# Attention over 16 images: row shifts of the scores by two DMAs through DRAM, maxima of every fourth query

## The chip, the cores and the metric

One Trainium2 chip, one of its cores. The time is the device time of that core in microseconds (us) for one execution of the whole program, all 16 images; the median of several executions counts. Where a profile is read, times are from the start of its span.

## What is computed

For each of 16 images (1024 tokens of 512 channels): group norm in 32 groups, SiLU, a projection to q, k and v (8 heads of 64), softmax attention for each head over all 1024 tokens, an output projection, a bias, and the image added again. Cut to what matters:

```
xn = silu(group_norm(x, scale, offset))              # b, 32, 32, 512
q, k, v = split(einsum('bxyc,cd->bxyd', xn, w_qkv))  # 8 heads of 64
q = q * 64 ** -0.5
attn = softmax(einsum('bhdi,bhdj->bhij', q, k), axis=-1)
out = einsum('bhij,bhdj->bhid', attn, v)
out = einsum('bxyd,dc->bxyc', out, w_out) + b_out
return out + x
```

## The kernel before

Products are made in fp16 halves: a value is kept as a high fp16 and a low fp16 part, and the high and low terms are added by further matmuls. Scores stand as keys x queries, so the maximum of a query's row of scores can't be taken from them. The kernel therefore makes a cheap copy of the scores ahead, queries x keys, from the high parts alone, and takes each query's maximum from it. The maximum, negated and scaled, is then fed into the score matmuls as one more operand: 64 rows of the moving operand `QK2` hold the shift of each query, against 64 stationary rows that hold the constant `ROWC`, and so exp() gets shifted scores.

The work of an image is 64 units of TensorE work (`UNITS`), in 4 steps of 16 (`step`, u = 0 to 15); v = 16 x step + u. A head has 8 units: 4 for queries 0 to 511 (half 0) and 4 for queries 512 to 1023 (half 1). In every unit TensorE does, in program order:

- `scores` (L1107, L1108): four matmuls of 512 columns into one of two PSUM buffers `ST`. At every fourth unit it first waits for the shift of its half (L1103);
- `turn`, in nine units of the 64: transposes;
- in even units `times_v` (L1137, 18 short matmuls for probabilities times v, two units behind), then a block of maxima (L1019), then the first half of a side job (L1005, a projection of q, k, v or out, six matmuls); in odd units the block of maxima, the other half of the side job, and `times_v` last;
- the shift, when there is one, at the very end of the odd unit.

A block of maxima is two matmuls of 512 columns into the PSUM tile `TP`, 128 queries x 1024 keys. It runs `TOP_LEAD` = 6 units ahead of its head. VectorE reduces it to one column of `mx` (L782). There is one `TP`, so each use of it waits until VectorE drained the one before (L1011). After the fourth block of a half (u = 1, 5, 9 or 13) VectorE makes the column form of the shift, `ms` (L752, 128 x 4). TensorE, at the end of the same unit, waits for it and turns the four columns into rows by four matmuls with `ident16` into `TP` (L1026). VectorE copies 64 rows of that, 64 x 512, into `QK2` (L786), at the start of its next unit. The first scores that need it are three units behind the block of maxima: the fourth block of half 0 comes in unit 8h - 3 and its scores in unit 8h, the one of half 1 in 8h + 1 and 8h + 4. So 16 shifts for an image, 256 in all.

VectorE also takes the low part of half of the probabilities (L835, every unit; GpSimd takes the other half, L509), drains the side jobs (L723, L728, L735), and does the norm and half of the SiLU of the next image, mostly in step 2 (L796, L825, L828). ScalarE takes two exponentials a unit (L620, L623).

SyncE issues all DMAs, in the order of its own program: `load_x` (L367), `load_res` (L373), `store` (L379), `place` (L390) and `move_v` (L396), each behind its waits. An instruction that waits holds all that stand behind it. `place` issues six DMAs of 256 KB each that lay the q and k of the next two heads from `QK` into `QK1` and `QK2`; it stands at u = 7 of each step and waits for the side job that VectorE drains in unit 8. The maxima of the next pair of heads, from u = 10, wait for its first three.

`Count` follows the counts of the semaphores through the order of the uses; `TOPS` are the uses of `TP`.

Of the kernel before, what the change touches and what calls it, by code (L numbers as in the profile page):

```python
# [13 lines left out]
P = 128  # L14
# [6 lines left out]
HALF = 512  # L21
# [34 lines left out]
def unit_max(step, u, last=False):  # L56

    head, qb = divmod(16 * step + u + TOP_LEAD, TB)
    return [] if last and head == HEADS else [("max", head // 2 % 4, head % 2, qb)]


def unit_shift(step, u, last=False):

    return [("shift", pair, hh, qb // 4) for _, pair, hh, qb in unit_max(step, u, last) if qb % 4 == 3]
# [8 lines left out]
def shift_before(step, u, last=False):  # L73

    if u > 0:
        return unit_shift(step, u - 1, last) + unit_stats(step, u - 1, last)
    return unit_shift(step - 1, 15, last) + unit_stats(step - 1, 15, last) if step > 0 else []

# [56 lines left out]
def image_of(use, b, step):  # L135
# [3 lines left out]
    if use[0] == "out" or (use[0] == "ot" and step == 0):  # L139
# [3 lines left out]

JOBS_PROLOGUE = [("qk", 0, "qk"[i % 2], i // 2) for i in range(4)] + [("v", t) for t in range(TB)]
PROLOGUE = ([("mean",), ("var",)] + JOBS_PROLOGUE[:4]
            + [use for t in range(TB) for use in [("v", t)] + ([("shift", 0, 0, 0)] if t == 6 else [])
               + ([("max", 0, 0, t - 2)] if t >= 2 else [])])
TOPS = ("max", "shift", "mean", "var")
IMAGE_JOBS = [x for s in range(4) for u in range(0, 16, 2) for x in unit_job(s, u)]
HI_PARTS = ("qk", "v")  # L150

# [1 line left out]
class Count:  # L153


    PER_IMAGE = {"side": len(IMAGE_JOBS), "hi": sum(x[0] in HI_PARTS for x in IMAGE_JOBS),
                 "top": HEADS * (TB + 2) + 2, "shifts": 2 * HEADS}

    def __init__(self, side=0, hi=0, top=0, shifts=0, ring=0, mark=None, shifted=(0, 0)):
        self.side, self.hi, self.top, self.shifts, self.ring = side, hi, top, shifts, ring  # L160
        self.shifted = list(shifted)
        self.mark = dict(mark or {"qk": 0, "v": 0})

    def passed(self, use):
        if use[0] in TOPS:
            self.top = self.top + 1
            if use[0] == "shift":
                self.shifts = self.shifts + 1
                self.shifted[use[3]] = self.top
# [12 lines left out]
    def later(self, images):  # L182

        n = {name: images * per for name, per in self.PER_IMAGE.items()}

        return Count(self.side + n["side"], self.hi + n["hi"], self.top + n["top"], self.shifts + n["shifts"],
                     self.ring, {kind: at + n["side"] for kind, at in self.mark.items()},
                     [at + n["top"] for at in self.shifted])


assert len(ring_of()) % 2 == 0 and B % 2 == 0
# [8 lines left out]
def conv_attention(nc, x, gamma, beta, w_qkv, w_out, b_out, out):  # L200
# [4 lines left out]
    with ctx:  # L205
# [11 lines left out]
        ident16 = sb("ident16", [P, P], F16)  # L217
# [56 lines left out]
        x_first = [x_in[:], z[:], th[:], Ph[:, 0:2, :].rearrange("p a n -> p (a n)").bitcast(F32).rearrange(  # L274
            "p (t c) -> p t c", t=2)]

        ST = ps("ST", [P, 2, 2 * HALF], F32)
        PV = ps("PV", [P, 512], F32)
        SD = ps("SD", [P, 512], F32)
# [44 lines left out]
        xn_lo = sem("xn_lo")  # L324
        v_moved = sem("v_moved")
        shift_ready = sem("shift_ready")
        scores_ready = sem("scores_ready")
        exp_done = sem("exp_done")
        lo_dve = sem("lo_dve")
# [19 lines left out]
        def _(sp):  # L349
# [31 lines left out]
            def place(pair, cnt):  # L381
# [15 lines left out]

            def step(b, s, cnt, first=False, last=False):
                for u in range(16):
                    if u % 2 == 0:  # L400
                        for use in unit_job(s, u, first, last):
                            cnt.passed(use)
                    if s == 0 and not last:
                        if u == 0 and first:
                            load_x(b + 1, 0)
                        if u in (1, 3, 7):
                            load_x(b + 1, (1, 3, 7).index(u) + 1)
                    if s == 0 and u == 4:
                        move_v(b)
                    if s == 1 and u == 0 and not first:  # L410
                        load_res(b - 1, 7)
                    if s == 2 and u == 4:
                        for t in range(4):
                            load_res(b, t)
                    if u == 7 and not (last and s == 3):
                        place((s + 1) % 4, cnt)
                    if s == 3 and u == 14 and not isinstance(b, int):
                        load_x(b + 2, 0)
                    if u % 2 == 1:
                        for use in unit_job(s, u, first, last):  # L420
                            if use[0] == "out":
                                store(b - 1, use[1], cnt.side)
                                if 1 <= use[1] <= 3:
                                    load_res(b - 1, use[1] + 3)

            cnt = Count()
            for use in JOBS_PROLOGUE:
                cnt.passed(use)
                if use == ("qk", 0, "k", 1):
                    place(0, cnt)  # L430
            step(0, 0, cnt, first=True)
            step(0, 1, cnt, first=True)
            with nc.Fori(0, B // 2 - 1, engines=[sp.engine], hint_back_edge=True) as two:
# [259 lines left out]
        def _(dve):  # L693
# [61 lines left out]
            def top_use(use, image, cnt):  # L755
# [12 lines left out]
                elif use[0] == "var":  # L768
# [11 lines left out]
                elif use[0] == "max":  # L780
# [65 lines left out]
            def step(b, s, par, cnt, first=False, last=False):  # L846
                turned = []
                for u in range(16):
                    v = 16 * s + u
                    if (s, u) == AGGREGATE_AT and not last:  # L850
                        dve.wait_ge(bn_done, b + 2)
                    for use in (shift_before(s, u, last) if not (first and v == 0) else []):
# [31 lines left out]
            nc.vector.tensor_copy(ident16[:], ident32[:])  # L884
# [114 lines left out]
        def _(pe):  # L999
# [9 lines left out]
            def top_use(use, image, cnt):  # L1009

                wait(pe, top_drained, cnt.top)  # L1011
                if use[0] == "max":
                    _, pair, hh, qb = use
                    slot = head_slot(pair, hh)
                    if qb == 0:

                        pe.wait_ge(placed[hh], PLACED * (4 * image + pair + 1))
                    for kh in range(2):
                        ins = nc.tensor.matmul(TP[:, bass.ts(kh, HALF)], QK1[:, slot, 0, bass.ts(qb, P)],  # L1019
                                               QK1[:, slot, 1, bass.ts(kh, HALF)], start=True, stop=True)  # L1020
                if use[0] == "shift":
                    _, pair, hh, half = use
                    pe.wait_ge(shift_ready, cnt.shifts + 1)
                    for i in range(4):
                        qb = 4 * half + i
                        ins = nc.tensor.matmul(TP[:, bass.ts(i, P)], ms[:, hh, qb:qb + 1].to_broadcast([P, P]),  # L1026
                                               ident16[:], start=True, stop=True)
                if use[0] == "mean":
                    pe.wait_ge(chan_stats, image + 1)
                    ins = nc.tensor.matmul(TP[:, 0:CC], group_mean[:], mv[:, :, 0], start=True, stop=True)  # L1030
# [63 lines left out]
                else:  # L1094
                    pe.wait_ge(ot_lo, 4 * (b - 1 if n == 3 else b) + n + 1)

            def scores(b, v, slot, cnt):
# [43 lines left out]
            def step(b, s, par, cnt, first=False, last=False):  # L1141
                for u in range(16):
                    v = 16 * s + u
                    before = (b, v - 2) if v >= 2 else (b - 1, UNITS + v - 2)
                    wait_ring(("score", v), b, first, last)
                    scores(b, v, cnt.next_slot(), cnt)
                    for use in unit_turn(s, u, first, last):
                        wait_ring(use, b, first, last)
                        turn(use, image_of(use, b, s), cnt.next_slot(), x_in)
# [7 lines left out]
                    else:  # L1157
# [81 lines left out]
```

## Time and profile before

| | us |
|---|---|
| median of 3 runs | 3889.32 |
| lowest and highest | 3886.81 and 3890.93 |
| the profiled execution, its own time | 3886.07 |
| its span, first to last instruction | 3884.3 |

Of the profile the page's busy shares of the engines matter, the view of waits (who waited for whom, in total and how many times), the groups of instructions by line and form (busy, mean ns of one, idle time of the engine before them), the timelines of TensorE (PE), its weight loads (PEld), VectorE (DVE) and SyncE's DMA queue (SPq), the windows (busy time of each engine in a stretch), and the DMAs with their time from issue to landing. The rows themselves stand below.

### The profile page before, as it was taken

To read this page: it belongs to the slowest core of one execution; us is meant where nothing else is said; L and a number is where in the kernel's file an instruction comes from. 1 tells how busy PE (TensorE), PEld (TensorE's weight loads), DVE (VectorE), ACT (ScalarE), POOL (GpSimd) and SP (SyncE) were. 2 spreads that over 40 slices of the span, in tenths; PEclk is the share of its full clock that TensorE was granted. 3 is DMA by queue.
4 is the path that set the end of the run, shared out by engine and by line. 5 is a ranking of instruction groups with operands and counts; after the bars stand their busy time and mean duration, and the time that the engine had idled before them with its cause. 6 is when DMAs were issued, how large, how long until landed. Compare 5 with 4: busy or idle time off the path is not lost. (4 is left out here: it accounts for less than half of the span.)

```text
span 3884.3 us, 92365 instructions
## 1 busy us (share of the span) xinstructions
PE 3643.0 (94%) x32844; PEld 2099.6 (54%) x32844; DVE 3349.9 (86%) x4378; ACT 2811.0 (72%) x3074; POOL 1766.9 (45%) x1739
## 2 busy tenths in 40 slices
PE   4889999999999999999999999999999999998997
PEld 2555555555555555555555555555555555555553
DVE  6888989889898898888888898888988989888885
ACT  3777777777777777777777777777777777777774
POOL 1353544445444444544535444344444444444444
PEclk7999999999999999999999999999999999999999
DMA  2212212132121222213122121221212222131220
GB/s 89 60 30 80 58 49 70 33 88 56 50 78 39 67 56 69 58 39 86 37 80 59 49 69 38 81 56 50 77 39 67 56 69 58 40 85 37 61 61 33
DMA packets 120769, 228.84 MB, mean 59 GB/s; under 512 B 12672, under 2 KB 29056, under 8 KB 120320
## 3 DMA queue, kind: packets, MB, share of 16 engines
q1 hardware_dynamic: 120320, 222.87, 21.2%
q8 instruction: 279, 4.57, 0.5%
q14 instruction: 170, 1.39, 0.1%
HBM read 71.57 MB, written 33.55 MB: 27 GB/s over the span
## 5 line engine op out<-in xcount | busy, mean ns | idle before, releaser
L509 POOL TENSOR_TENSOR Pl<-P,Ph 128x512 f16<-128x512 f32 x1024 | 1238.3, 1209 | 1703.9 <-ACT Ph L623 1691.0
L620 ACT ACTIVATE P<-ST,cns 128x1024 f32<-128x1024 f32 x1024 | 1141.0, 1114 | 899.3 <-PE ST L1108 883.4
L782 DVE TENSOR_REDUCE mx<-TP 128x1 f32<-128x1024 f32 x1024 | 1246.3, 1217 | 164.5 <-PE TP L1019 156.8
L623 ACT ACTIVATE Ph<-ST,cns 128x1024 f16<-128x1024 f32 x1024 | 1133.8, 1107 | 0.0
L835 DVE TENSOR_TENSOR Pl<-P,Ph 128x512 f16<-128x512 f32 x1024 | 978.8, 956 | 11.5 <-ACT Ph L623 7.3
L1137 PE MATMUL PV<-V,Ph 128*128 128x129 f16 (+2 forms) x10240 | 862.1, 210 | 3.9 <-DVE Pl L835 1.4
L1137 PEld LDWEIGHTS PV<-V,Ph 128*128 128x128 f16 x10240 | 772.0, 97 | 124.9 <-ACT pv_sum L631 8.8
L1137 PE MATMUL PV<-V,Pl 128*128 128x65 f16 x8192 | 834.8, 192 | 0.0
L1137 PEld LDWEIGHTS PV<-V,Pl 128*128 128x128 f16 x8192 | 723.0, 98 | 109.1 <-issue 0.6
L1108 PE MATMUL ST<-QK 128*128 128x512 f16 x2048 | 778.2, 380 | 2.6 <-issue 2.6
L1107 PE MATMUL ST<-QK 128*128 128x512 f16 x2048 | 778.6, 380 | 0.2 <-ACT Ph L623 0.2
L1005 PE MATMUL SD<-X,wq 128*128 128x512 f16 x3048 | 745.5, 381 | 15.9 <-POOL X L496 15.2
L1019 PE MATMUL TP<-QK 128*128 128x512 f16 x2048 | 611.0, 380 | 27.7 <-DVE QK L786 13.7
L1005 PEld LDWEIGHTS SD<-X,wq 128*128 128x128 f16 x3048 | 291.1, 98 | 395.4 <-DVE QK L723 34.9
L1005 PE MATMUL SD<-wo,OT 128*128 128x512 f16 x1536 | 376.8, 383 | 44.8 <-DVE QK L723 27.4
L1005 PE MATMUL SD<-wq,X 128*128 128x512 f16 x1488 | 361.6, 379 | 10.2 <-DVE V L728 7.2
L1107 PEld LDWEIGHTS ST<-QK 128*128 128x128 f16 x2048 | 202.8, 99 | 184.1 <-issue 3.0
L1108 PEld LDWEIGHTS ST<-QK 128*128 128x128 f16 x2048 | 200.6, 98 | 182.4 <-issue 2.5
L1005 PEld LDWEIGHTS SD<-wo,OT 128*128 128x128 f16 x1536 | 145.8, 98 | 244.9 <-DVE res L735 39.0
L786 DVE CAST QK<-TP 64x512 f16<-64x512 f32 x256 | 176.1, 688 | 116.5 <-PE TP L1026 113.7
L723 DVE SCALAR_TENSOR_TENSOR QK<-SD,sc,QK 128x512 f16<-128x512 f32 x254 | 190.0, 748 | 91.6 <-ACT QK L577 75.0
L519 POOL TENSOR_TENSOR O<-pv_sum,den 128x256 f32<-128x256 f32 x256 | 157.8, 616 | 239.8 <-DVE pv_sum L843 239.8
(105 smaller groups left out, 2872.8 us busy)
## 6 DMA issues: line engine op xcount, KB each, us to landing
QK<-QK SPq DMA_DIRECT2D x384, 256.0 KB, 4.8
res<-in_x SPq DMA_DIRECT2D x128, 256.0 KB, 2.8
out<-res SPq DMA_DIRECT2D x128, 256.0 KB, 2.0
x_in<-in_x SPq DMA_DIRECT2D x61, 512.0 KB, 3.8
V<-V SPq DMA_DIRECT2D x16, 1040.0 KB, 6.3
V<-in_L_conv_w_qkv SPq DMA_DIRECT2D x4, 768.0 KB, 10.2
P<-in_L_conv_w_out SPq DMA_DIRECT2D x1, 1024.0 KB, 13.9
z<-in_x SPq DMA_DIRECT2D x1, 512.0 KB, 5.6
```

Of the source, the lines that this page charges most:

```text
L509: nc.gpsimd.tensor_tensor(Pl[:, v % 4, HALF:], P32[:, v % 2, HALF:], Ph[:, v % 4, HALF:], ALU.subtract).then_inc(lo_pool, 1)
L620: nc.scalar.activation(P32[:, v % 2, :], ST[:, slot, :], ACT.Exp, scale=cns[:, 0:1])
L623: nc.scalar.activation(Ph[:, v % 4, :], ST[:, slot, :], ACT.Exp, scale=cns[:, 0:1]).then_inc(exp_done, 1)
L723: nc.vector.scalar_tensor_tensor(out=QK[:, lo, cols], in0=bank, scalar=sc[:, col:col + 1], in1=QK[:, hi, cols], op0=ALU.mult, op1=ALU.subt ...
L782: nc.vector.reduce_max(mx[:, hh, qb:qb + 1], TP[:], AX.X).then_inc(top_drained, 1)
L786: nc.vector.tensor_copy(QK2[r, head_slot(pair, hh), 0, bass.ts(half, HALF)], TP[r, 0:HALF]).then_inc(top_drained, 1)
L835: nc.vector.tensor_tensor(Pl[:, v % 4, 0:HALF], P32[:, v % 2, 0:HALF], Ph[:, v % 4, 0:HALF], ALU.subtract).then_inc(lo_dve, 1)
L1005: ins = nc.tensor.matmul(bank, stationary(i, c), moving(j, c), start=(c == 0 and i + j == 0), stop=(c == CC - 1 and i == 1))
L1019: ins = nc.tensor.matmul(TP[:, bass.ts(kh, HALF)], QK1[:, slot, 0, bass.ts(qb, P)], QK1[:, slot, 1, bass.ts(kh, HALF)], start=True, stop=True)
L1107: nc.tensor.matmul(dst, QK1[:, at, 1, kb], QK1[:, at, 0, bass.ts(q, HALF)], start=True, stop=False)
L1108: ins = nc.tensor.matmul(dst, QK2[:, at, 1, kb], QK2[:, at, 0, bass.ts(q, HALF)], start=False, stop=True)
L1137: ins = nc.tensor.matmul(PV[:, cols], stationary, moving, start=kb == qb == n == 0, stop=kb == TB - 1, skip_group_check=True)
```

## The change

The shift no longer goes over TensorE, PSUM and VectorE. The uses `shift` of `TP` go, with their four matmuls, the copy L786, `ident16` and the counts kept for them. SyncE, once `ms` is there, writes the four columns of `ms` into a row of 512 fp16 in DRAM (128 pieces of 8 bytes), waits for that, and reads the row from DRAM into the 64 rows of `QK2` (64 rows of 1 KB). The scores wait for the second DMA in place of the copy. It stands in SyncE's program at the unit in which the fourth block of the half is made.

So that the row in DRAM is in the order of the queries when partition p writes its four values side by side, a block of maxima now holds every fourth query of its half: partition p of block i is query 4p + i. The stationary operand of the two matmuls of a block is thus read with a step of four elements instead of one.

```
 def place_shift(b, n):                                   # new, SyncE
     head, half = n // 2 % HEADS, n % 2
     pair, hh = head // 2, head % 2
     sp.wait_ge(shift_ready, 2 * HEADS * b + n + 1)
     sp.dma_start(rows[half].rearrange("(p j) -> p j", j=4), ms[:, hh, 4 * half:4 * half + 4]
                  ).then_inc(shift_row[half], 16)
     sp.wait_ge(shift_row[half], 16 * HEADS * b + 16 * (n // 2) + 16)
     sp.dma_start(QK2[rows_of(1 - hh), head_slot(pair, hh), 0, bass.ts(half, HALF)],
                  rows[half:half + 1].to_broadcast([HD, HALF])).then_inc(shift_placed[half], 16)
```

```
@@ SyncE, step @@
                 if s == 3 and u == 14 and not isinstance(b, int):
                     load_x(b + 2, 0)
+                for n in unit_shift(s, u, last):
+                    place_shift(b, n)
                 if u % 2 == 1:
@@ VectorE, top_use @@
-                else:
-                    _, pair, hh, half = use
-                    r = rows_of(1 - hh)
-                    nc.vector.tensor_copy(QK2[r, head_slot(pair, hh), 0, bass.ts(half, HALF)], TP[r, 0:HALF]
-                                          ).then_inc(top_drained, 1)
@@ TensorE, top_use @@
-                        ins = nc.tensor.matmul(TP[:, bass.ts(kh, HALF)], QK1[:, slot, 0, bass.ts(qb, P)],
+                        ins = nc.tensor.matmul(TP[:, bass.ts(kh, HALF)],
+                                               QK1[:, slot, 0, qb // 4 * HALF + qb % 4:(qb // 4 + 1) * HALF:4],
                                                QK1[:, slot, 1, bass.ts(kh, HALF)], start=True, stop=True)
-                if use[0] == "shift":
-                    _, pair, hh, half = use
-                    pe.wait_ge(shift_ready, cnt.shifts + 1)
-                    for i in range(4):
-                        qb = 4 * half + i
-                        ins = nc.tensor.matmul(TP[:, bass.ts(i, P)], ms[:, hh, qb:qb + 1].to_broadcast([P, P]),
-                                               ident16[:], start=True, stop=True)
@@ TensorE, scores @@
-                    pe.wait_ge(top_drained, cnt.shifted[q])
+                    pe.wait_ge(shift_placed[q], 16 * HEADS * b + 16 * head + 16)
@@ TensorE, step, end of odd units @@
-                        for use in unit_shift(s, u, last):
-                            top_use(use, b, cnt)
```

## Rows read from the trace of the kernel before

**Rows 1.** Page: span, busy time of the engines, granted TensorE clock in 40 slices.

```profile
span 3884.3 us, 92365 instructions
...
PE 3643.0 (94%) x32844; PEld 2099.6 (54%) x32844; DVE 3349.9 (86%) x4378; ACT 2811.0 (72%) x3074; POOL 1766.9 (45%) x1739
...
PEclk7999999999999999999999999999999999999999
```

**Rows 2.** View of waits, whole span: us in total, times, longest.

```profile
PE TP L1026 <- DVE ms L752: 98.0, 98, 3.0
...
PE TP L1019 <- DVE QK L786: 13.7, 30, 1.9
PE TP L1019 <- DVE mx L782: 12.6, 16, 2.0
```

**Rows 3.** Groups by form: count | busy us, mean ns | idle before, by whom ended.

```profile
L786 DVE CAST QK<-TP 64x512 f16<-64x512 f32 x256 | 176.1, 688 | 116.5 <-PE TP L1026 113.7
...
L1019 PEld LDWEIGHTS TP<-QK 128*128 128x128 f16 x2048 | 157.4, 97 | 156.2 <-DVE mx L782 52.9 <-DVE QK L786 17.4 <-issue 1.0
...
L1079 PEld LDWEIGHTS ST<-ident,O 128*128 128x128 f32 x512 | 61.1, 144 | 17.9 <-issue 3.4 <-POOL O L519 2.0 <-ACT Ph L623 1.0
```

**Rows 4.** TensorE's timeline at a shift without a wait: start, length in us.

```profile
2001.62 0.19 PE L1137 MATMUL PV<-V,Pl 128*128 128x65 f16 x1
2001.67 0.40 PE L1026 MATMUL TP<-ident,ms 128*128 128x128 f16 x4
2001.90 0.38 PE L1107 MATMUL ST<-QK 128*128 128x512 f16 x1
2002.12 0.38 PE L1108 MATMUL ST<-QK 128*128 128x512 f16 x1
```

**Rows 5.** TensorE's timeline in step 2, from u = 5 to u = 8.

```profile
2116.41 0.59 PE L1019 MATMUL TP<-QK 128*128 128x512 f16 x2
...
2120.41 0.40 PE L1026 MATMUL TP<-ident,ms 128*128 128x128 f16 x4 [1.39 <-DVE ms L752]
...
2127.24 0.38 PE L1107 MATMUL ST<-QK 128*128 128x512 f16 x1
```

**Rows 6.** VectorE's timeline at the same shift.

```profile
2118.11 1.22 DVE L782 TENSOR_REDUCE mx<-TP 128x1 f32<-128x1024 f32 x1
2119.37 0.98 DVE L752 TENSOR_SCALAR ms<-mx,cns 128x4 f16<-128x4 f32 x1
2120.84 0.68 DVE L786 CAST QK<-TP 64x512 f16<-64x512 f32 x1 [0.49 <-PE TP L1026]
```

**Rows 7.** Windows: a stretch of step 2; length, then PE, PEld, DVE, ACT, POOL busy.

```profile
2134.00:2150.00 16.00, 14.66 (x145) 8.43 (x144) 15.24 (x19) 12.97 (x16) 7.11 (x7) 1.00 0.26 62
```

**Rows 8.** DMA issues: count, KB each, median us from issue to landing.

```profile
res<-in_x SPq DMA_DIRECT2D x128, 256.0 KB, 2.8
out<-res SPq DMA_DIRECT2D x128, 256.0 KB, 2.0
...
bet<-in_L_conv_gn_offset SPq DMA_DIRECT2D x1, 2.0 KB, 3.8
```

**Rows 9.** SyncE's timeline in step 1: the six DMAs of `place`, and a store.

```profile
2069.97 5.93 SPq L390 DMA_DIRECT2D QK<-QK  x6
2076.40 0.88 SPq L379 DMA_DIRECT2D out<-res  x1
```

**Rows 10.** Landing of the sixth DMA of that `place`, issued at 2074.72.

```profile
L390 SPq DMA_DIRECT2D QK<-QK x1: 1186/1186/1186, 2074.7 to 2074.7; - x1
...
DMA to landing us min/median/max: 5.4/5.4/5.4
```

**Rows 11.** Landing of that store.

```profile
DMA to landing us min/median/max: 4.3/4.3/4.3
```

**Rows 12.** VectorE's timeline in step 1, u = 9.

```profile
2074.07 0.23 DVE L752 TENSOR_SCALAR ms<-mx,cns 128x4 f16<-128x4 f32 x1
```

**Rows 13.** TensorE's timeline in step 1: first scores of u = 12.

```profile
2081.43 0.38 PE L1107 MATMUL ST<-QK 128*128 128x512 f16 x1
```

More of the change, by code:

```diff
@@ L62, in unit_shift, with head_of @@
 def unit_shift(step, u, last=False):
-    return [("shift", pair, hh, qb // 4) for _, pair, hh, qb in unit_max(step, u, last) if qb % 4 == 3]
+    return [2 * head_of(step, u) + qb // 4 for _, pair, hh, qb in unit_max(step, u, last) if qb % 4 == 3]
+def head_of(step, u):
+    return (16 * step + u + TOP_LEAD) // TB
 def unit_stats(step, u, last=False):
@@ L70, in unit_stats, with stats_before @@
     return [(kind,)] if kind and not last else []
[L73 to L77, printed above, removed]
+def stats_before(step, u, last=False):
+    return unit_stats(step, u - 1, last) if u > 0 else unit_stats(step - 1, 15, last) if step > 0 else []
 JOBS = [["qk"] * 4 + ["out"] * 4, ["qk"] * 4 + ["out"] * 4, ["qk"] * 4 + ["v"] * 4, ["qk"] * 4 + ["v"] * 4]
@@ L145 @@
 PROLOGUE = ([("mean",), ("var",)] + JOBS_PROLOGUE[:4]
-            + [use for t in range(TB) for use in [("v", t)] + ([("shift", 0, 0, 0)] if t == 6 else [])
-               + ([("max", 0, 0, t - 2)] if t >= 2 else [])])
-TOPS = ("max", "shift", "mean", "var")
+            + [use for t in range(TB) for use in [("v", t)] + ([("max", 0, 0, t - 2)] if t >= 2 else [])])
+TOPS = ("max", "mean", "var")
 IMAGE_JOBS = [x for s in range(4) for u in range(0, 16, 2) for x in unit_job(s, u)]
@@ L156, with __init__ @@
     PER_IMAGE = {"side": len(IMAGE_JOBS), "hi": sum(x[0] in HI_PARTS for x in IMAGE_JOBS),
[L157 to L161, printed above, removed]
+                 "top": HEADS * TB + 2}
+    def __init__(self, side=0, hi=0, top=0, ring=0, mark=None):
+        self.side, self.hi, self.top, self.ring = side, hi, top, ring
         self.mark = dict(mark or {"qk": 0, "v": 0})
@@ L166, in passed @@
             self.top = self.top + 1
-            if use[0] == "shift":
-                self.shifts = self.shifts + 1
-                self.shifted[use[3]] = self.top
             return
@@ L184, in later @@
         n = {name: images * per for name, per in self.PER_IMAGE.items()}
-        return Count(self.side + n["side"], self.hi + n["hi"], self.top + n["top"], self.shifts + n["shifts"],
-                     self.ring, {kind: at + n["side"] for kind, at in self.mark.items()},
-                     [at + n["top"] for at in self.shifted])
+        return Count(self.side + n["side"], self.hi + n["hi"], self.top + n["top"], self.ring,
+                     {kind: at + n["side"] for kind, at in self.mark.items()})
 assert len(ring_of()) % 2 == 0 and B % 2 == 0
@@ L275, in conv_attention @@
             "p (t c) -> p t c", t=2)]
+        rows = nc.dram_tensor("shift_rows", (2, HALF), F16, kind="Internal").ap()
         ST = ps("ST", [P, 2, 2 * HALF], F32)
@@ L326, in conv_attention @@
         shift_ready = sem("shift_ready")
+        shift_row = [sem(f"shift_row{half}") for half in range(2)]
+        shift_placed = [sem(f"shift_placed{half}") for half in range(2)]
         scores_ready = sem("scores_ready")
@@ L430, in _ @@
                     place(0, cnt)
+            place_shift(0, 0)
             step(0, 0, cnt, first=True)
@@ L779, in top_use @@
                                             ALU.mult, ALU.add).then_inc(guess_ready, 1)
-                elif use[0] == "max":
+                else:
                     _, pair, hh, qb = use
                     nc.vector.reduce_max(mx[:, hh, qb:qb + 1], TP[:], AX.X).then_inc(top_drained, 1)
-                else:
-                    _, pair, hh, half = use
-                    r = rows_of(1 - hh)
-                    nc.vector.tensor_copy(QK2[r, head_slot(pair, hh), 0, bass.ts(half, HALF)], TP[r, 0:HALF]
-                                          ).then_inc(top_drained, 1)
                 cnt.passed(use)
@@ L851, in step @@
                         dve.wait_ge(bn_done, b + 2)
-                    for use in (shift_before(s, u, last) if not (first and v == 0) else []):
+                    for use in stats_before(s, u, last):
                         top_use(use, b + 1, cnt)
@@ L883, in _ @@
             dve.wait_ge(const_ready, 5)
-            nc.vector.tensor_copy(ident16[:], ident32[:])
             dve.wait_ge(gn_loaded, 32)
@@ L1018, in top_use @@
                     for kh in range(2):
-                        ins = nc.tensor.matmul(TP[:, bass.ts(kh, HALF)], QK1[:, slot, 0, bass.ts(qb, P)],
+                        ins = nc.tensor.matmul(TP[:, bass.ts(kh, HALF)],
+                                               QK1[:, slot, 0, qb // 4 * HALF + qb % 4:(qb // 4 + 1) * HALF:4],
                                                QK1[:, slot, 1, bass.ts(kh, HALF)], start=True, stop=True)
-                if use[0] == "shift":
-                    _, pair, hh, half = use
-                    pe.wait_ge(shift_ready, cnt.shifts + 1)
-                    for i in range(4):
-                        qb = 4 * half + i
-                        ins = nc.tensor.matmul(TP[:, bass.ts(i, P)], ms[:, hh, qb:qb + 1].to_broadcast([P, P]),
-                                               ident16[:], start=True, stop=True)
                 if use[0] == "mean":
@@ L1095, in wait_ring, with scores @@
                     pe.wait_ge(ot_lo, 4 * (b - 1 if n == 3 else b) + n + 1)
-            def scores(b, v, slot, cnt):
+            def scores(b, v, slot):
                 head, q, kp = v // 8, v // 4 % 2, v % 4
@@ L1145, in step @@
                     wait_ring(("score", v), b, first, last)
-                    scores(b, v, cnt.next_slot(), cnt)
+                    scores(b, v, cnt.next_slot())
                     for use in unit_turn(s, u, first, last):
```

1 line of the change is left out of this document (removed).

## The prediction

> **What bounds the kernel now.** I read the page first: the reader is to see that TensorE is busy for 94% of the span at the full granted clock, and VectorE for 86% [rows 1]. So TensorE's order sets the time, and what matters is its own work and its 241 us of idle time (3884.3 - 3643.0). Then the view of waits: of that idle time 98.0 us in 98 pieces is spent at the shift, waiting for `ms`, the largest single entry; another 13.7 us in 30 pieces is a block of maxima that waits for the copy of the shift out of `TP` [rows 2]. Then the timelines around shifts. In one without a wait the four matmuls push the next scores back by 0.23 us (2001.67 to 2001.90) [rows 4]. In one with a wait TensorE has nothing to do for 1.39 us [rows 5], because VectorE reached the block of maxima late: reduce at 2118.11, `ms` ready at 2120.35, 3.9 us after the block's matmuls began at 2116.41 [rows 5, 6]. Last the windows: in a 16 us stretch of step 2 VectorE is busy 15.24 us and TensorE 14.66 [rows 7]. There VectorE is no spare engine but nearly a second bound.
>
> **What goes from TensorE.** (a) 256 shifts at 0.23 us: 59 us [rows 3, 4]. (b) The wait for `ms`, 98 us, and with each of these 98 pieces the tail of the last matmul before it: that one is drawn 0.19 us long while its successor would start 0.05 us later, so a break costs 0.14 us more than its idle time; 98 x 0.14 = 14 us [rows 2, 4]. Together 112. (c) The blocks that wait for the copy: 13.7 us + 30 x 0.14 = 18 us [rows 2, 4]. The sum is 189 us.
>
> **What goes from VectorE.** 256 copies of 688 ns, 176 us, and 116.5 us in which it stood before them, waiting for TensorE's four matmuls [rows 3]. That is 1.1 us at each shift on average. By itself it is worth nothing, as VectorE is not the bound over most of the image, but it decides how much of (b) lasts. After (b) TensorE no longer waits for a late VectorE at `ms`; the next place where it can be late is the next block of maxima, which needs the same `TP` drained. There TensorE is ahead by 0.23 + 0.14 + the wait of about 1.0 us, 1.4 us in all, and VectorE by 0.68 + 0.49 = 1.17 us at a shift such as the one shown [rows 2, 4, 6]. The difference, 0.2 to 0.3 us, can come back as a wait: 98 x 0.3 = 29 us. I take the 29, with 0 as the low end (a stall of TensorE elsewhere lets VectorE catch up) and 60 as the high end.
>
> **What the new path costs.** Nothing of it runs on TensorE or VectorE; it is latency behind `ms` and in front of the scores three units on. Both ends of that interval have rows. `ms` ready at 2120.35, scores at 2127.24: 6.9 us [rows 5, 6]. Ready at 2074.30, scores at 2081.43: 7.1 us [rows 12, 13]. In the middle images no shift has less. With the change the scores come earlier by the 0.23 us of the four matmuls, and by the wait of that shift with its 0.14: 6.9 - 0.23 - 1.39 - 0.14 = 5.1 us for the worst, 6.9 us for the second.
>
> The chain has two DMAs. The first writes 1 KB to DRAM in 128 pieces; the nearest rows are the stores to DRAM, 2.0 us for 256 KB, and from above the 3.8 us of `bet`, 512 pieces of 4 bytes that was issued right behind a 512 KB load [rows 8]. I take 2.0, because the time of a small DMA is latency and `bet` had a load before it. The second reads 64 KB from DRAM; the nearest row is `res<-in_x` with 2.8 us for 256 KB, four times as much [rows 8]; I take 2.3, bounds 2.0 and 2.8. With 0.1 us for SyncE to go on, the chain is 4.4 us (bounds 4.1 and 6.7). It fits into 5.1 us and more: twelve of the sixteen shifts of an image are hidden. If the cover is gone, each 0.1 us over it costs 0.1 us of TensorE.
>
> The other four, at u = 9 of each step, meet `place`. Its six DMAs are issued over 5.93 us from 2069.97, and the sixth (2074.72) lands 5.4 us later, at 2080.1 [rows 9, 10]. A store issued at 2076.40, which alone takes 2.0 us, took 4.3 us and landed at 2080.7, 0.6 us behind the sixth [rows 8, 9, 11]: the queue is served in its order. The first DMA of the shift will do the same: landed at 2080.7, second issued 2080.8, landed 2083.1, but wanted at 2081.43 - 0.23 = 2081.2. A stall of 1.9 us. That is the worst of the four; in steps 0, 2 and 3 the same reckoning, averaged over the middle images, gives 0.1, 0.9 and 1.1 us, and 1.6 for step 1: 3.7 us an image, 58 us in all. Bounds: 30 us with 2.0 us for each DMA and 0.3 us behind `place`, 100 us with 2.5 and 2.8.
>
> What is queued behind the waits on SyncE: SyncE now waits inside `place_shift` for `ms` and for the first DMA, 2 us or 4 at u = 9. Behind it stand stores and loads of `res` with many us of cover, `load_x` (in step 3 it now goes behind two shifts, some 3 us before its transposes), and `place`, three units behind the shift of u = 5, which is done in about half of that. I cost these at nothing; the cover is one to two units of about 3.5 us each.
>
> The strided weights: a block's weight load takes 97 ns, hidden under matmuls of 512 columns; no row has a strided one. The nearest is the fp32 load, 144 ns [rows 3]. Up to the 0.22 us from one matmul of 512 columns to the next [rows 4] it stays hidden except the first load behind the short matmuls of `times_v`, in even units: 512 x (144 - 97) ns = 24 us at most. I take 0, since the fp32 load moves twice the bytes and this one the same. A gain is excluded: no read becomes shorter. The Trainium skill speaks against this edit on one page (TensorE: Matmul & The Clock Gate, section Weight-path perf modes): a fast weight load reads 32 bits at a time, two fp16 values, and with a step of four only one of the two is wanted. The same table lets strided chunks keep the mode, which is what I take; no row here shows it. On the DMA pair the page DMA: Bandwidth & Descriptors (Anatomy of one DMA) gives about 2.0 us plus bytes / 436 GB/s; an estimate by it is 4.2 us for the chain, against 4.4 by the rows, and its specifications say that pieces under 512 B are read, changed and written again, which would lengthen the first.
>
> **The sum**, against the profiled execution's 3886.1 us (2 us over its span): 3886 - 189 + 29 + 58 = 3784. The median of the runs lies 3 us above the profiled one, so I say 3786.
>
> **The rivals.** 1. All of the chain is hidden, because stalls and VectorE's lag overlap and the DMAs are quick: 3886 - 189 + 0 + 12 to 30, 3709 to 3727. For it: two DMAs at 2.0 us leave the queue's tail as the only cost. Against: [rows 9 to 11] show that tail at 0.6 us more. 2. The gain mostly given back: first DMA 3.0, second 2.8, 1 us behind `place`. Then also the shifts in steps 2 and 3 with 5.1 to 5.5 us are late; 147 us of stalls, 3886 - 189 + 147 + 10 = 3854. 3. Slower: the first DMA is like `bet`, 3.8 us (or 2 us behind `place`), the second 2.8, 6.7 us in all. At u = 9 TensorE then stalls for 2.8 us on average and at the other twelve for 0.4: 16 x (4 x 2.8 + 12 x 0.4) = 256 us, less 189: 3953. It turns from gain to loss where the lone chain reaches about 6.0 us. For it: 8-byte pieces, which no row shows. Against: the latency of 2.0 us for 256 KB. 4. The strided load is slow: each load above 215 ns is bare twice in a block. It needs (215 + 102 / 2048 x 1000 = 265) ns a load to eat the gain; at 390, four times today's, 2048 x 175 ns = 358 us, so 4140. No row is near it. 5. VectorE becomes the bound of step 2 and TensorE's waits only move to blocks and side jobs: (b) lasts for the 34 waits outside step 2 alone, so about 64 x 1.1 = 70 us more come back: 3854. Against: VectorE loses 1.1 us at each shift too. 6. That the change doesn't take the four matmuls away: excluded by the diff.
>
> **How the numbers follow.** Forecast (3750 to 3820) 0.60; rival 1 0.12; rivals 2 and 5 (3820 to 3875) 0.16; rival 3 0.07; rival 4 0.03; about no change, between 2 and 3, 0.02. The likeliest alone gives 3750 to 3820; the range that holds 8 in 10 takes in part of rivals 1 and 2 and the bounds 30 and 100 us of the queue: 3728 to 3855. About 0.2% (8 us) is what a measurement here can tell from no change. Faster 0.88, same 0.03, slower 0.09.
>
> **What would show it.** The waits for `ms` and for L786 gone; TensorE busy 3643 less about 75 us; VectorE less 176. A new entry "scores wait for a DMA", some 64 times, 58 us, at u = 12 alone, with the landing of the second DMA 10 to 13 us after `place` begins. The first DMA at 2.0 us from issue to landing where the queue is empty, the second at 2.3. Weight loads of L1019 still near 97 ns. Waits of blocks for the reduce at 15 to 45 us. I am wrong if scores wait at u = 0, 4 or 8 too (chain over 5.1 us), if weight loads take over 200 ns, or if the waits for the reduce grow by over 60 us.

## The result, and the profile after

The changed kernel takes 3927.65 us (median of 4 runs, 3920.91 to 3932.88) against 3888.07 us before in the same comparison: 1.010 times as long, 95% interval 1.008 to 1.012. The forecast was 3786, the range 3728 to 3855. The sign was wrong, and the difference is clear of the noise: what happened is the third rival, at a smaller size than its 3953.

The page after, answering to [rows 1], the chain that ended last with it:

```profile
span 3931.1 us, 90267 instructions
...
PE 3640.7 (93%) x31820; PEld 2057.4 (52%) x31820; DVE 3182.3 (81%) x4121; ACT 2805.2 (71%) x3074; POOL 1749.0 (44%) x1739
...
PE 47%; DMA 19%; DVE 13%; issue 8%; SPq 7%; ACT 6%; ACTq 0%; POOL 0%; DVEq 0%; POOLq 0%
```

VectorE lost 168 us of work, where 176 were expected. TensorE issues 1024 matmuls less and is drawn as busy for as long as before. DMA and SyncE's queue hold a quarter of the chain that ended last (the page before follows its chain over less than a tenth of the span, so there is no share to set beside it). The view of waits (us in total, times, longest), answering to [rows 2], says where:

```profile
PE ST L1109 <- DMA QK<-shift_rows: 154.9, 114, 4.7
...
PEld PV L1139 <- ACT pv_sum L646: 79.8, 196, 0.5
```

The 98.0 us for `ms` and the 13.7 us for the copy are gone. In their place the scores wait 154.9 us for the second DMA, 114 times. The second line will matter below; the same wait in the kernel before:

```profile
PEld PV L1137 <- ACT pv_sum L631: 8.8, 34, 0.3
```

The DMAs (count, KB each, median us from issue to landing), answering to [rows 8]:

```profile
QK<-shift_rows SPq DMA_DIRECT2D x256, 64.0 KB, 3.2
shift_rows<-ms SPq DMA_DIRECT2D x256, 1.0 KB, 3.0
```

3.0 and 3.2 us, where the forecast had 2.0 and 2.3. The lone chain (both DMAs where the queue is empty) is 6.2 us, not 4.4, and it was said that the change turns to a loss at about 6.0.

One chain at its worst place, step 1, u = 9, to the scores of u = 12. SyncE's queue, TensorE and VectorE, with start and length in us:

```profile
1866.24 5.95 SPq L390 DMA_DIRECT2D QK<-QK  x6
1872.30 1.25 SPq L398 DMA_DIRECT2D shift_rows<-ms  x1
1876.93 0.48 SPq L401 DMA_DIRECT2D QK<-shift_rows  x1
```

```profile
1868.45 0.62 PE L1028 MATMUL TP<-QK 128*128 128x512 f16 x2
...
1879.95 0.38 PE L1109 MATMUL ST<-QK 128*128 128x512 f16 x1 [1.09 <-DMA QK<-shift_rows]
```

```profile
1870.37 0.23 DVE L767 TENSOR_SCALAR ms<-mx,cns 128x4 f16<-128x4 f32 x1
```

`ms` is ready at 1870.60. SyncE is still issuing `place`, and gets to the shift at 1872.30. The first DMA lands 4.6 us later, at 1876.9, the second at 1879.8, and the scores start at 1879.95, 11.5 us behind the block of maxima at 1868.45. Before it was 9.3 us at the same place, from this block to the scores of [rows 13]:

```profile
2072.17 0.59 PE L1019 MATMUL TP<-QK 128*128 128x512 f16 x2
```

Over twelve images of the middle, read from the timelines in the same way, mean us for each of the 16 shifts (v: the unit of the scores; block to ms: from the start of the block to the start of `ms`; ms to issue: from its end, 0.2 us later):

```
   v   block to ms   ms to issue   first DMA   second DMA   idle before scores
  12      2.49          0.03         4.39        3.16          1.25   u = 9
  28      1.91          1.71         4.67        3.08          2.26   u = 9
  44      2.20          0.46         4.82        3.30          1.42   u = 9
  60      1.98          0.97         4.75        3.09          1.69   u = 9
  36      3.47          0.03         3.06        3.69          0.73
  40      3.80          0.03         2.95        2.99          0.41
  52      3.81          0.03         2.92        2.98          0.48
  other nine: 1.9 to 2.6  0.03     2.9 to 3.2   2.9 to 3.8     0.05 or less
```

In these images the idle time is 8.3 us each. Four fifths of it is at u = 9, behind `place`; most of the rest where VectorE is late.

The first and the last image have more. The same wait in the windows 0:338 and 3663:3931.2, about the first and the last image:

```profile
PE ST L1109 <- DMA QK<-shift_rows: 18.8, 9, 4.7
PE ST L1109 <- DMA QK<-shift_rows: 22.2, 8, 4.5
```

In the last image 17.7 us of that fall on its last five shifts (v = 44 to 60), 2.7 to 4.5 us each. In the kernel before, where TensorE waited for `ms`, it was ready 5.0 to 5.2 us ahead of the scores there, against 6.9 and more in the middle; in the changed kernel it is 3.2 us and less, the stall taken off. In the first image the largest two, 4.7 and 4.4 us, are at v = 12 and 28, where it was 5.0 us before.

### The profile page after: what moved, and what is told of

Its sections match the earlier page's. It is cut to its first block, busy times and chain, and to the rows that moved or that the text cites. A ratio compares the mean times of both kernels' runs of the same rounds, so it can differ in the third digit from the quotient of the medians.

```text
span 3931.1 us, 90267 instructions
## 1 busy us (share of the span) xinstructions
PE 3640.7 (93%) x31820; PEld 2057.4 (52%) x31820; DVE 3182.3 (81%) x4121; ACT 2805.2 (71%) x3074; POOL 1749.0 (44%) x1739
## 4 chain that ended last, share of the span: by engine, by line
PE 47%; DMA 19%; DVE 13%; issue 8%; SPq 7%; ACT 6%; ACTq 0%; POOL 0%; DVEq 0%; POOLq 0%
PE SD L1013 18%; DMA shift_rows<-ms 10%; PE PV L1139 8%; DMA QK<-shift_rows 8%; SPq L390 7%; PE ST L1109 6%; PE ST L1110 6%; PE TP L1028 5%; DVE mx L797 4%; DVE QK L738 2%; DVE Pl L845 2%; ACT Ph L638 2%; ACT QK L592 2%; PE ST L1075 1%; PE ST L1082 1%
## 5 line engine op out<-in xcount | busy, mean ns | idle before, releaser
L524 POOL TENSOR_TENSOR Pl<-P,Ph 128x512 f16<-128x512 f32 x1024 | 1218.6, 1190 | 1761.8 <-ACT Ph L638 1749.7
L845 DVE TENSOR_TENSOR Pl<-P,Ph 128x512 f16<-128x512 f32 x1024 | 1005.5, 982 | 13.7 <-ACT Ph L638 9.6
L1109 PE MATMUL ST<-QK 128*128 128x512 f16 x2048 | 782.2, 382 | 155.6 <-DMA QK<-shift_rows 154.9
L1139 PE MATMUL PV<-V,Ph 128*128 128x129 f16 (+2 forms) x10240 | 872.1, 211 | 13.9 <-ACT pv_sum L646 4.2
L1028 PE MATMUL TP<-QK 128*128 128x512 f16 x2048 | 619.5, 384 | 11.3 <-DVE mx L797 9.4
L1028 PEld LDWEIGHTS TP<-QK 128*128 128x128 f16 x2048 | 183.2, 115 | 130.1 <-DVE mx L797 53.7
```

Source lines behind the costliest of these rows:

```text
L524: nc.gpsimd.tensor_tensor(Pl[:, v % 4, HALF:], P32[:, v % 2, HALF:], Ph[:, v % 4, HALF:], ALU.subtract).then_inc(lo_pool, 1)
L845: nc.vector.tensor_tensor(Pl[:, v % 4, 0:HALF], P32[:, v % 2, 0:HALF], Ph[:, v % 4, 0:HALF], ALU.subtract).then_inc(lo_dve, 1)
L1109: nc.tensor.matmul(dst, QK1[:, at, 1, kb], QK1[:, at, 0, bass.ts(q, HALF)], start=True, stop=False)
L1139: ins = nc.tensor.matmul(PV[:, cols], stationary, moving, start=kb == qb == n == 0, stop=kb == TB - 1, skip_group_check=True)
```

## The experiments

The kernel before was run beside these, with medians of 3887.5 to 3889.6 us; the ratios are to it.

Theory A: the loss is the latency of the chain in front of the scores, and it has three parts, the two DMAs' own length, the queue behind `place`, and the late `ms` of step 2. Rivals: the strided weight load costs (C); another engine is next and the stalls are no cause (B).

**The strided load alone.** On the kernel before, whose shifts thus stand at other queries of the same half:

```
-  nc.tensor.matmul(TP[:, bass.ts(kh, HALF)], QK1[:, slot, 0, bass.ts(qb, P)],
+  nc.tensor.matmul(TP[:, bass.ts(kh, HALF)],
+                   QK1[:, slot, 0, qb // 4 * HALF + qb % 4:(qb // 4 + 1) * HALF:4],
```

> The kernel before with one edit: a block of maxima is every fourth query, so its weight loads have a step of four. The shifts still go over TensorE in the old order, so they stand at other queries of the same half; the output is the softmax with another shift, which is left as it is. Theory A (the strided load costs next to nothing): the weight load of the block 97 -> 112 ns as in the changed kernel, 5 ns more for 512 blocks behind short matmuls, +3 us: 3888 to 3895. Theory C (the strided load is a good part of the 40 us lost): 3910 or more.

3888.86 us against 3888.67, ratio 1.000 (0.999 to 1.001). The weight load, groups by form (busy, mean ns), answering to the second of [rows 3]:

```profile
L1019 PEld LDWEIGHTS TP<-QK 128*128 128x128 f16 x2048 | 183.6, 115 | 148.8 <-DVE mx L782 51.2 <-DVE QK L786 17.4 <-issue 1.0
```

A load has become 18 ns longer, and the time is the same. C falls.

**No wait.** Both DMAs are issued, but their result isn't used; the rows of the shift hold zeros, so no shift is applied:

```
 sp.dma_start(
-    QK2[rows_of(1 - hh), head_slot(pair, hh), 0, bass.ts(half, HALF)],
+    spare[rows_of(1 - hh), half, :],
...
-    pe.wait_ge(shift_placed[q], 16 * HEADS * b + 16 * head + 16)
+    wait(pe, shift_placed[q], 16 * HEADS * b + 16 * head)
```

> The changed kernel with both DMAs issued as before, but the second goes to a spare tile, and the scores wait for that of one head earlier, which has landed long ago. The shift rows hold zeros (no shift is applied; the output is softmax without one). SyncE's queue and its waits are unchanged. Theory A (the stalls in front of the scores are all of the loss): 152 us of stalls go and nothing comes back beyond the 28 us of times_v waiting after scores and 12 us of side jobs: 3770 to 3790. Theory B (VectorE or ScalarE is next): over 3850. It also shows what remains of the gain that I forecast for TensorE alone.

3742.22 us, ratio to before 0.962 (0.961 to 0.964). The wait costs 3928 - 3742 = 186 us, more than the 155 us drawn as idle. In the middle images one takes 10.0 us longer with the wait than without; 9.5 of that is a longer way from `times_v` to the scores, the stall with the tail of the matmul before it. That is 160 us in 16 images, and 26 us more lie in the first and the last. B falls: nothing else takes the stalls' place. SyncE's DMAs, all of them, cost nothing that can be seen as long as nobody waits.

Part of the 186 us is the clock. The granted clock, mean over the span, is 0.993 here, 0.990 in the kernel before and 0.984 in the changed one. As it is either 2.4 or 1.2 GHz, an estimate from these means and the spans is 52, 78 and 126 us at the lower level. In the changed kernel TensorE went on at 442.91 after standing 2.42 us for the second DMA; in the stretch from 444.90 to 446.80 the granted clock was 0.50, and two matmuls of 512 columns at 444.97 took 0.84 us to the next start, against 0.46 at 1868.45, where it was 1.00. So at most half of 126 - 52 = 74 us, 37 of the 186, is work done more slowly behind stalls and not time spent standing, and at most half of 126 - 78 = 48 us, 24 of the 40 us lost. The clock by itself doesn't make the loss: in the run "Another row" below it is 0.985, nearly that of the changed kernel, and the time is that of the kernel before.

**One DMA.** The row in DRAM is written once, at the start, and read for every head, so all heads get the first one's shifts:

```
 sp.wait_ge(shift_ready, 2 * HEADS * b + n + 1)
-sp.dma_start(rows[half].rearrange("(p j) -> p j", j=4), ms[:, hh, 4 * half:4 * half + 4]
-             ).then_inc(shift_row[half], 16)
-sp.wait_ge(shift_row[half], 16 * HEADS * b + 16 * (n // 2) + 16)
```

> The changed kernel without the first of the two DMAs: the row in DRAM is written once at the start and read for every head, so all heads get the shifts of the first one (the output isn't the reference's softmax shift). It takes 3.0 us off the chain where the queue is empty (6.2 -> 3.2 us). Theory A (the length of the chain is what costs): the twelve clear shifts of an image are hidden, of the four at u = 9 the queue's tail stays, the stalls fall from 152 us to 20 to 40: 3800 to 3825. Theory B (TensorE only waits for another engine instead, the stalls are no cause): over 3880.

3751.46 us, 0.965 (0.963 to 0.967), 49 us better than the lower end that A expected. The stalls are gone in the middle images, at u = 9 too:

```profile
PE ST L1112 <- DMA QK<-shift_rows: 6.4, 4, 3.9
```

A single DMA that stands behind `place` still lands in time. With two, the second can't start before the first has come through the queue, and it is the one that is late. The read by itself took 2.5 us (median), near the 2.3 I had taken.

**The row in SBUF.** One partition of SBUF in place of DRAM:

```
-rows = nc.dram_tensor("shift_rows", (2, HALF), F16, kind="Internal").ap()
+rows = sb("rows", [P, 2, HALF], F16)
```

> The changed kernel with the row of 512 shifts in one partition of SBUF in place of DRAM; both DMAs keep their pieces. If DRAM is what makes the DMAs 3.0 and 3.2 us long (my 2.0 and 2.3 were wrong by that), the first falls to 2.0 to 2.4 and the second to 2.2 to 2.8, and the time to 3860 to 3890. If it is the 128 small pieces and the 64 rows, they keep 3.0 and 3.2 us and the time stays at 3920 to 3935.

3919.40 us, 1.008 (1.006 to 1.010). Both expectations were half right:

```profile
QK<-rows SPq DMA_DIRECT2D x256, 64.0 KB, 3.9
rows<-ms SPq DMA_DIRECT2D x256, 1.0 KB, 1.9
```

The same 128 pieces of 8 bytes take 1.9 us into SBUF and 3.0 us into DRAM, so for the first DMA the target makes the difference of 1.1 us, and not the number of pieces. The second became longer, 3.9 us, where its 64 reads all go to one partition. The chain is 5.8 us instead of 6.2, and TensorE got 8 us back.

**Another row.** The second DMA reads a row that was written at the start, everything else as in the changed kernel:

```
 sp.dma_start(QK2[rows_of(1 - hh), head_slot(pair, hh), 0, bass.ts(half, HALF)],
-             rows[half:half + 1].to_broadcast([HD, HALF])).then_inc(shift_placed[half], 16)
+             still[half:half + 1].to_broadcast([HD, HALF])).then_inc(shift_placed[half], 16)
```

> The changed kernel; the second DMA reads another row in DRAM, written once at the start (so all heads get the first one's shifts), while the first is issued and waited for as before. With one DMA alone the read took 2.5 us, in the changed kernel 3.2. If reading a row that was written just before costs the 0.7 us, the read falls to 2.5 us here, and the time to 3870 to 3900. If it is the queue's state or anything else, it stays at 3.2 us and 3920 to 3935.

3886.48 us, 1.000 (0.998 to 1.001), the read at 2.5 us:

```profile
QK<-still_rows SPq DMA_DIRECT2D x256, 64.0 KB, 2.5
shift_rows<-ms SPq DMA_DIRECT2D x256, 1.0 KB, 3.0
```

So 0.7 us of the 3.2 are the price of reading the row of DRAM that was written just before, and not of the queue's state; why, these runs don't say. That alone is 41 us of time, all of the loss. With a lone chain of 3.0 + 2.5 = 5.5 us the change neither gains nor loses, and with the 5.8 us of the row in SBUF it still loses: the measured turning point is near 5.5 us, not 6.0.

**Place split.** In SyncE's program the last three DMAs of `place`, which nobody needs for some 35 us, go behind the shift of u = 9:

```
 if u == 7 and not (last and s == 3):
-    place((s + 1) % 4, cnt)
+    place((s + 1) % 4, cnt, (0,))
...
 for n in unit_shift(s, u, last):
     place_shift(b, n)
+if u == 9 and not (last and s == 3):
+    place((s + 1) % 4, cnt, (1,))
```

> The changed kernel; of the six DMAs of place the last three, which the second head of the pair needs some 35 us later, are issued behind the shift of u = 9 instead of ahead of it. Theory A (at u = 9 the shift's first DMA stands in the queue behind place): at u = 9 the first DMA falls from 4.4 to 4.8 us to about 3.0, SyncE's delay ahead of it in steps 1 and 3 (1.7 and 1.0 us) goes, and of 6.6 us of stalls an image at u = 12 about 1 is left, so 80 us less: 3780 to 3850, faster than the kernel before. If instead the lone chain of 6.2 us is by itself too long everywhere, the stalls move to the other units and the time stays over 3890.

3818.67 us, 0.982 (0.980 to 0.983): 109 us from one order of issue. At u = 9 the first DMA takes 3.0 to 3.3 us, SyncE issues it 0.03 us behind `ms` in all steps, and the idle time there falls from 6.6 us an image to 0.1:

```profile
PE ST L1111 <- DMA QK<-shift_rows: 66.7, 60, 4.6
```

What is left, 66.7 us, is 2.7 us in an image of the middle, nearly all at v = 36, 40 and 52 (1.0, 0.6 and 1.0 us), where `ms` comes 3.5 to 3.8 us behind its block, and 30 us in the first and last image. My expectation had 1 us an image left at u = 9, and it is 0.1. (The profiled execution took 3829.6 us, 11 more than the median.)

**Split, and the row in SBUF.** Both edits together:

> The changed kernel with place split as in the run before (3819 us) and the row of shifts in one partition of SBUF in place of DRAM (first DMA 1.9 us in place of 3.0, second 3.9 in place of 3.2: a chain of 5.8 us in place of 6.4). Split alone left 3.3 us of stalls an image in front of the scores, at v = 36, 40 and 52 most of all, where ms comes 3.5 to 3.8 us after its block. Theory A (each 0.1 us of the chain over its cover is paid by TensorE): 0.3 to 0.6 us less at each of these three and nothing elsewhere: 3790 to 3812. If the stalls are not set by the chain, 3819 stays.

3789.99 us, 0.975 (0.974 to 0.976), the fastest kernel here that leaves nothing out: 98 us under the kernel before. At v = 36, 40 and 52 the idle time is 0.0, 0.2 and 0.4 us, 0.98, 0.33 and 0.65 less than with the row in DRAM. The two DMAs together are 1.1, 0.3 and 0.6 us shorter there: about one for one, as A has it. The 1.96 us an image are 31 us in 16, and the time fell by 29.

**The four matmuls alone.** On the kernel without a wait, four matmuls of 128 columns where the shift's stood, ahead of the next unit's scores:

```
 wait_ring(("score", v), b, first, last)
+for _ in unit_shift(s, u - 1, last) if u > 0 else []:
+    for i in range(4):
+        nc.tensor.matmul(ST[:, cnt.ring % 2, bass.ts(i, P)], wo[:, 0, i, 0:P], wo[:, 0, 0, 0:P],
+                         start=True, stop=True)
```

> The changed kernel whose scores don't wait for the shift (3742 us; the shift rows hold zeros, as there), with four matmuls of 128 columns put where the four of the shift stood before, ahead of the scores of the next unit; what they write is overwritten. If the four matmuls cost TensorE their 0.22 us each time, as I reckoned, 256 x 0.22 = 57 us more: 3799. If most of it is taken back because times_v of that next unit waits for ScalarE's copy of PV anyway (1.4 us an image in excess between scores and times_v in the run without waits, none in the kernel before), 57 - 22 = 35 us more: 3770 to 3785, and that excess is gone.

3749.00 us, 0.964 (0.963 to 0.966): 7 us over the 3742 without them. I had expected 35 us. The matmuls are there, 1020 of them (four of one shift fewer than before), and nothing waits ahead of them:

```profile
L1152 PE MATMUL ST<-wo 128*128 128x128 f16 x1020 | 98.3, 219 | 0.0
```

and the waits show who had taken their place (first the kernel without them, then with them):

```profile
PEld SD L1015 <- DVE QK L739: 113.9, 163, 2.3
PEld PV L1141 <- ACT pv_sum L647: 76.8, 196, 0.5
```

```profile
PEld SD L1015 <- DVE QK L739: 95.3, 163, 2.3
...
PEld PV L1141 <- ACT pv_sum L647: 18.6, 70, 0.3
```

In starts of TensorE's work, twelve images of the middle: without the four, `times_v` begins 1.8 us an image later behind the scores and transposes, and the side job 1.7 us later behind the block of maxima; the blocks begin 0.3 us earlier behind `times_v`. That is 3.2 us an image, 51 over 16, of the 57 that the four were to cost. In the unit after an odd one, TensorE reaches `times_v` before ScalarE's copy of PV is done, and the next side job before ScalarE and VectorE have drained the last one. The four matmuls stand ahead of both, in time that is idle anyway. That is measured between two kernels without waits for `ms`; in the kernel before, where such waits stand in the same place, their worth was not measured by itself.

**The shift later, by TensorE.** On the kernel before, the four matmuls behind the scores of the next unit:

```
 scores(b, v, cnt.next_slot(), cnt)
+for use in shifts_due(s, u, last):     # the shift of unit u - 1
+    top_use(use, b, cnt)
```

> The kernel before (no DMA for the shift), with the four shift matmuls moved from the end of the odd unit to behind the scores of the next unit, 0.86 us later. If the wait for ms (98 us, 1.0 us each) is most of the gain that a shift off TensorE's order can bring, moving it behind 0.86 us of work takes 70 to 80 of the 98 us, less what blocks then wait for the copy (13.7 us before, up to 30 more): 3800 to 3860. Rival: VectorE is as late at the next block, and the wait only moves there: 3880 to 3900.

3903.31 us, 1.003 (1.002 to 1.004), a small loss: the rival, 3 us beyond its 3880 to 3900. The wait for `ms` fell from 98.0 to 30.2 us, and with the tails the way through the scores and the shift to `times_v` became 4.6 us an image shorter. But the way from `times_v` to the block of maxima, which now finds `TP` still in use by the shift, grew by 3.5 us an image, and that from the block to the side job by 2.1: 89 us more against 74 less in 16 images. With one `TP` the shift's way through PSUM costs either at its start or at its end.

**VectorE's block first.** On the split kernel with the row in SBUF, VectorE takes the fourth block and `ms` ahead of its low probabilities from step 2 on (`early` is true in the units of a fourth block there):

```
+for use in unit_max(s, u, last) if early else []:
+    top_use(use, b + 1, cnt)
 if not (first and v == 0):
     low_probs(b, v - 1)
...
-for use in unit_max(s, u, last):
+for use in unit_max(s, u, last) if not early else []:
     top_use(use, b + 1, cnt)
```

> As the first kernel of this job, and VectorE, from step 2 on, in the units with the fourth block of a half takes the block and ms ahead of its half of the low probabilities. If VectorE's lateness in step 2 (ms 3.5 to 3.8 us behind its block, against 1.9 elsewhere) is what is left of the stalls, ms comes 0.7 us or more earlier and the stalls at v = 36, 40 and 52 go: 3760 to 3790. If TensorE then waits for the low probabilities instead, no gain or a loss: 3800 or more.

3804.20 us, 0.979 (0.978 to 0.980), 14 us worse than without. `ms` came only 0.0 to 0.5 us earlier at v = 36, 40 and 52; the idle time there is gone, but TensorE waits for the low probabilities instead:

```profile
PE PV L1144 <- DVE Pl L847: 50.8, 52, 1.9
```

## Why the prediction was wrong, by its steps

**What bounds the kernel** held: TensorE's order. The two runs without the wait are at 96 and 97% busy.

**(a), the four matmuls, 59 us: mis-sized, it is 7 us** as the filler run has it. I measured how far they push the next scores back, which is right, and did not ask what stands behind them. The prediction did ask that of the wait, not of the work. The cover was in the trace: `times_v` comes 0.9 us behind the shift's end and needs ScalarE's copy of PV, and the 8.8 us in 34 pieces of that wait before said that it was close.

**(b) and (c), the waits, 112 + 18 us, less 29 us for VectorE: 101 forecast.** The filler run has the four matmuls and neither the waits nor VectorE's copies: 3888 - 3749 = 139 us. The 130 us of waits were sized well; the 29 us that VectorE was to take back did not appear: TensorE's waits of blocks for the reduce are 12.6 us before, 9.4 in the changed kernel and 13.7 in the filler run. So what the change takes away was forecast at 160 us and is 146 (3888 - 3742). That this is close is luck: (a) was 52 us too high, and waits and VectorE together 38 us too low.

**The chain, 4.4 us: the step that failed.** It is 6.2 us, and the stalls in front of the scores, forecast at 58 us, cost 186. The first DMA was taken from the stores, 2.0 us for 256 KB to DRAM; 128 pieces of 8 bytes take 3.0 there and 1.9 in SBUF. The text had `bet` with its 3.8 us on the other side and explained it away by the load ahead of it. The second was taken as 2.3, and a lone read takes 2.5; the 0.7 us for a row written just before stands in no row of the kernel before. "One DMA" and "Another row" show what these durations are worth: without the first DMA (and with the read at 2.5 us) the time is 176 us lower, with the second one 0.7 us shorter it is 41 us lower.

With 6.2 us the worst cover of the forecast, 5.1 us, is passed by 1.1, and the scores at v = 36, 40 and 52 stall, 1.6 us an image, which the text had named as the sign of being wrong. The real covers there are 5.6 to 6.2 us, which is why each stall is only 0.4 to 0.7 us.

The Trainium skill's figure for the chain, an estimate of 4.2 us by DMA: Bandwidth & Descriptors (Anatomy of one DMA), is low as well; that section measures DMAs that GpSimd issues, and these are SyncE's. What the page's specifications say of pieces under 512 B pointed the right way, but the same pieces took 1.9 us into SBUF, so the size of the pieces alone doesn't make the 3.0 us.

**The queue at u = 9: the mechanism was right, the size wrong.** The first DMA does land 0.5 to 1.2 us behind `place` (0.6 forecast). 3.7 us an image were forecast and 6.6 came. The second DMA, 3.1 to 3.3 us there and not 2.3, makes 3.4 us in the four shifts together, more than the 2.9 that were missing. In steps 1 and 3 SyncE comes to the shift 1.0 to 1.7 us late, as it is still issuing `place`; the text doesn't say so, but its reckoning held it, since the store that it went by was issued behind `place` too: in step 1 the first DMA lands 6.4 us behind `ms` in the mean, as forecast (2080.7 - 2074.3). The split run shows the term by itself: 109 us.

**The first and last image: not in the sum.** The covers were taken from the middle images and counted 16 times. The first and the last image stall for 41 us of the 155, where the 3.7 us an image had 7, because `ms` is ready later before the scores there: 3.2 us and less at the last five shifts of the last image. Even a chain of 4.4 us would have stalled at those.

**SyncE's other work, at nothing:** right. With all DMAs issued and none waited for the time is 3742.

**The strided load, at nothing:** right, 3888.86. Its weight load takes 115 ns against 97. The reading that I took of the Trainium skill's TensorE: Matmul & The Clock Gate (Weight-path perf modes), that strided chunks keep the fast mode, is not contradicted by 115 ns; which mode ran no run here shows.

**VectorE** is down by 168 us, 176 forecast. **TensorE's busy time** did not fall by 75 us but by 2. Without the wait it is 3595.2 us, 48 less than before; the other 45 come back with the stalls, in part as matmuls at the lower clock are drawn longer. And a wait shorter than a drawn matmul's tail (0.38 us drawn, 0.22 to the next start: 0.16 us) counts as busy. It was no good measure of (a).

**The chances.** The loss had 0.09. The rival was worked out with its turning point at 6.0 us, and 6.2 came; between 4.4 and 6.0 us there were 1.6 us of margin for two durations, neither of which had a row of its own kind. That was worth far more than 0.07. That the turning point was so near is in part luck, as it left out the first and last image and the clock behind stalls; the runs put it near 5.5.

## What to carry to other kernels

A step taken off the bounding engine is worth what the engine finds behind it: before a matmul is counted as a gain, look at the next instruction's operand, and how late it comes. A chain of dependent DMAs on a shared queue is paid in latency, so place it by what the queue holds at that moment, and move what nobody waits for behind it; here that order was worth 109 us, nearly three times the loss. A cover that is read in the middle of a kernel has to be read again at its start and its end. And when a forecast stands on durations with no row of their own kind, the distance to the turning point is the confidence, not the story.

## What the runs showed of the hardware that I had not expected

- A DMA of 1 KB in 128 pieces of 8 bytes takes 3.0 us to DRAM and 1.9 us to one partition of SBUF.
- A read of 64 x 1 KB from one row of DRAM takes 2.5 us, and 3.2 us (median) right after that row was written; from one partition of SBUF, also written just before, 3.9 us.
- A weight load with a step of four fp16 elements takes 115 ns against 97; the time of the kernel is the same with it (ratio 1.000, 0.999 to 1.001).
- Six DMAs of 256 KB from SBUF to SBUF take SyncE 5.9 us to issue; what is ready meanwhile is issued up to 1.7 us late, and lands 0.5 to 1.2 us behind them (means of the four steps).
- Stalls of TensorE of up to 4.7 us, 8.3 us in an image of the middle, go with more time at the lower clock: a mean granted clock of 0.984, against 0.993 in the same kernel without the wait.
